# Weighted sums moved behind the bursts of scores in the attention part of a decoder layer

## The reference, cut to what matters

```python
x = layernorm(x + attn(x))        # 32 samples of 128 tokens, 1024 wide
x = layernorm(x + xattn(x, ctx))  # a 3-tap convolution gated by cosine similarities
x = layernorm(x + ffn(x))         # rank-16 experts mixed by a softmax router
# attn, 32 query heads over 8 key heads of 32 columns, for each sample:
q, k, v = x @ wq.T, x @ wk.T, x @ wv.T     # q and k are rotated by position
scores = q @ k.T / sqrt(32)                # causal mask
out = softmax(scores) @ v @ wo.T
```

## Time and profile before

| | us |
|---|---|
| median of three executions | 1433.07 |
| the profiled execution | 1434.46 |
| its span (first to last instruction) | 1432.60 |
| part 1, first loads and steps 0 to 2 (to 84.29) | 84.29 |
| part 1, steps 3 to 30, from a burst of scores at 84.29 to one at 714.38 | 630.09 |
| part 1, steps 31 to 33 (714.38 to 780.79) | 66.41 |
| part 2 (from 780.79 to the end) | 651.8 |

### The profile page before, as it was taken

One profiled execution on the slowest core, in us unless ns is written; L12 is line 12 of the kernel. 1 busy time (PEld: TensorE's weight loads), 2 busy tenths in 40 slices (PEclk: granted clock), 3 DMA queues, 4 the chain that ended last, 5 costly groups with the idle time before them and its releaser, 6 DMA issues. The chain is left out here.

```text
span 1432.6 us, 32298 instructions
## 1 busy us (share of the span) xinstructions
PE 1368.6 (96%) x8288; PEld 1060.1 (74%) x8288; DVE 1091.2 (76%) x3869; ACT 932.3 (65%) x3258; POOL 983.9 (69%) x936
## 2 busy tenths in 40 slices
PE   6999999999999999999985899999999999999995
PEld 4777777777777777777753688888888888888873
DVE  5677777777777777777775487788887788887774
ACT  5688878788787877878775354555554455554543
POOL 2777777777677776777764666777776777776763
PEclk9999999999999999999996999999999999999997
DMA  7345445454444544445466856655666766766651
GB/s 242 97 126 157 128 135 150 119 157 121 139 152 118 152 123 145 147 121 152 120 193 175 204 150 167 174 148 161 164 156 165 174 150 160 165 153 164 161 118 45
DMA packets 108861, 213.03 MB, mean 149 GB/s; under 512 B 26640, under 2 KB 32272, under 8 KB 108816
## 3 DMA queue, kind: packets, MB, share of 16 engines
q1 hardware_dynamic: 108624, 212.25, 53.9%
q10 hardware_dynamic: 192, 0.26, 0.1%
HBM read 131.83 MB, written 34.47 MB: 116 GB/s over the span
## 5 line engine op out<-in xcount | busy, mean ns | idle before, releaser
L435 PE MATMUL wo_ps<-weights,halves 128*128 128x512 f32 x2304 | 573.8, 400 | 11.8 <-DVE weights L614 11.7
L435 PEld LDWEIGHTS wo_ps<-weights,halves 128*128 128x128 f32 x2304 | 423.9, 190 | 128.6 <-issue 34.6
L697 ACT ACTIVATE pexp<-sm,smin 128x128 f32<-128x128 f32 x1024 | 398.8, 393 | 122.8 <-DVE smin L565 120.9
L1056 PE MATMUL wo_ps<-weights,halves 128*128 128x512 f32 x1488 | 400.9, 402 | 2.6 <-DVE yz L1159 2.6
L827 POOL TENSOR_TENSOR pn<-pexp,prec 128x512 f32<-128x512 f32 x256 | 268.6, 1049 | 146.9 <-DVE prec L572 146.9
L1409 POOL TENSOR_TENSOR prods<-prod,prods 128x512 fp32r<-128x512 f32 x192 | 259.3, 1358 | 134.5 <-ACT prods L1303 129.5
L1056 PEld LDWEIGHTS wo_ps<-weights,halves 128*128 128x128 f32 x1488 | 273.4, 190 | 61.6 <-issue 4.3
L565 DVE CUSTOM_DVE_ANT_0 sm<-s_ps,mask_t 128x128 f32<-128x128 f32 x1024 | 231.7, 281 | 78.7 <-PE s_ps L465 77.5
L1303 ACT CAST prods<-prod 128x512 fp32r<-128x512 f32 x192 | 118.8, 621 | 165.8 <-DVE prod L1193 129.2
L1193 DVE TENSOR_TENSOR prod<-att,x 128x512 f32<-128x512 f32 x192 | 187.0, 989 | 12.2 <-DMA att<-sim_scratch 9.7
L697 ACT ACTIVATION_READ_ACCUMULATOR pexp<-sm,smin 128x1 f32 x1024 | 194.8, 190 | 0.0
(11 more groups left out here) (99 smaller groups left out, 1661.2 us busy)
## 6 DMA issues: line engine op xcount, KB each, us to landing
att<-sim_scratch SPq DMA_DIRECT2D x192, 252.0 KB
pt<-blocks SPq DMA_DIRECT2D x636, 64.0 KB, 2.0
ctx_t<-in_ctx SPq DMA_DIRECT2D x32, 576.0 KB, 4.6
raw<-in_xT SPq DMA_DIRECT2D x32, 512.0 KB, 3.8
raw<-ot_scratch SPq DMA_DIRECT2D x32, 512.0 KB, 6.7
xn<-in_x SPq DMA_DIRECT2D x32, 512.0 KB, 7.4
out<-late SPq DMA_DIRECT2D x32, 512.0 KB, 6.2
ot_scratch<-ot SPq DMA_DIRECT2D x63, 256.0 KB, 2.1
```

Of the source, the lines that this page charges most:

```text
L435: mm = pe.matmul(qkv_ps[(par + g) % 2][:], xs[:, par, xl, k], w_sb[:, wl, g, k], start=(k == 0 and n == 0), stop=(k == KT - 1 and n == 2))
L697: ins = nc.scalar.activation(pexp[:, c % 2, i * P:(i + 1) * P], sm[:, c % 2, i * P:(i + 1) * P], ACT.Exp, bias=smin[:, c % 2, i:i + 1], sc ...
L1056: mm = pe.matmul(wo_ps[n][:], os_t[:, par, ol, k], wo_sb[:, wl, k, n * BANK:(n + 1) * BANK], start=(k == 0 and m == 0), stop=(k == KT - 1 ...
```

## The change

`weigh` moves. Half 0 of sample b goes from slot 9 to slot 13, directly behind the second burst of scores; half 1 goes from slot 17 to slot 1 of the next step, directly behind the first burst (there the sample is c = t-3). In steps 32 and 33 half 1 stays at slot 17, and half 0 is at slot 13 in them too.

ScalarE reads the sums one place later: at chunk 3 it reads half 1 of c (before: half 0 of b), at chunk 6 half 0 of b (before: half 1 of b). In steps 32 and 33 it reads half 1 at chunk 7.

SyncE's list follows: `move_v` of sample a goes from the end of step a to the next step, behind the loads of the next sample and its context; the store of half 0 goes to the end of the step and that of half 1 behind `move_p(b, 1)` of the next step; a wait for half 0 of the sums now stands ahead of the store of the context sums.

```diff
@@ move_p(a, u), on SyncE
-            wait(sp, pv_done, after(a - 1, NU, u + 1))
+            if u == 1:
+                wait(sp, pv_done, after(a - 1, NU, NU))
@@ step(t, par), on SyncE
+            a, b, c = t - 1, t - 2, t - 3
+            if at_step(t, 1):
+                move_v(0, 0)
...
+            if valid(a) and not at_step(t, 1):
+                move_v(a, 1 - par)
             if valid(b):
                 move_p(b, 1)
-                wait(sp, ot_read, after(b, NU, 1))
-                sp.dma_start(ot_dram[b, :, 0:BANK], ot[:, 0]).then_inc(ot_out[0], 16)
+            if valid(c) and not at_step(t, LAST):
+                store_later_half(c)
             if at_step(t, LAST):
                 store_own()
...
+            if valid(a):
+                wait(sp, pv_done, after(a - 1, NU, 1))
             if valid(t):
                 wait(sp, sq_done, after(t, 1, 1))
...
-                move_v(t, par)
...
-            if valid(b) and not at_step(b, B - 1):
-                wait(sp, ot_read, after(b, NU, 2))
-                sp.dma_start(ot_dram[b, :, BANK:D], ot[:, 1]).then_inc(ot_out[1], 16)
+            if valid(b):
+                wait(sp, ot_read, after(b, NU, 1))
+                sp.dma_start(ot_dram[b, :, 0:BANK], ot[:, 0]).then_inc(ot_out[0], 16)
+            if at_step(t, B):
+                store_later_half(b)
@@ step(t, par), on TensorE
-                if valid(b):
-                    if s == 9:
-                        weigh(b, par, 0)
-                    if s == 17:
-                        weigh(b, par, 1)
+                if s == 1 and valid(c) and not at_step(t, LAST):
+                    weigh(c, 1 - par, 1)
+                if s == 1 + NJ * PERIOD and valid(b):
+                    weigh(b, par, 0)
+                if s == 17 and (at_step(t, B) or at_step(t, LAST)):
+                    weigh(b, par, 1)
@@ step(t, par), on ScalarE
-                if p == 6 and at_step(t, LAST):
+                if p == 7 and at_step(t, LAST):
                     move_last_row()
...
-                if p == 3 and valid(b):
+                if p == 3 and valid(c) and not at_step(t, LAST):
+                    read_ot(c, 1)
+                if p == 6 and valid(b):
                     read_ot(b, 0)
-                if p == 6 and valid(b):
+                if p == 7 and (at_step(t, B) or at_step(t, LAST)):
                     read_ot(b, 1)
                 if p == 6 and valid(t):
                     copy_k(t, par)
```

More of the change, by code:

```diff
@@ L309, in move_p, with store_later_half @@
                                  ).then_inc(p_in[u], 16)
+        def store_later_half(b):
+            wait(sp, ot_read, after(b, NU, 2))
+            sp.dma_start(ot_dram[b, :, BANK:D], ot[:, 1]).then_inc(ot_out[1], 16)
         def load_later(n):
@@ L373, in step @@
         def step(t, par):
-            a, b = t - 1, t - 2
+            a, b, c = t - 1, t - 2, t - 3
+            if at_step(t, 1):
+                move_v(0, 0)
             if valid(t + 1):
```

## The result

The changed kernel took 1449.02 us (median of five, 1446.89 to 1450.13), the kernel before 1432.07 beside it: ratio 1.0123 (95% interval 1.0106 to 1.0140). It is slower, as forecast, but by 17.0 us and not by 9.6. A second set of five gave 1449.75 against 1432.48, ratio 1.0126 (1.0104 to 1.0147).

The account below looks back on a forecast made before the run. TensorE, never idle in steps 3 to 30, bounds the kernel. First steps -0.2, 28 steps +7.2, steps 31 to 33 +0.5, end of part 1 +2.05: +9.6 on 1433.07 gives 1442.7 us, range 1434 to 1449 (8 in 10).

Parts of the forecast that it names:

- TensorE's own list: TensorE's work in one step without waits: moving both halves of the sums changes it by 2x - 0.68, or -0.28 us.
- x: Distance from the last score matmul to the first of the moved sums: taken as 0.20 us, bounds 0.03 and 0.33.
- The stall at slot 22: Query transposes wait for ScalarE's key copy, which comes 1.00 later: TensorE idle 0.52 us a step, step 22.76.
- `copy_q`: ScalarE's query copy ahead of the first burst of scores: 0.70 us of cover left, costs nothing.
- the barrier: End of part 1: last sums' store now issued behind the similarities, its landing awaited before part 2: +2.05 us, once.
- `move_v` behind the context load: Values queue behind two large loads in each step; VectorE waits 0.5 to 1.0 us for them, hidden, price 0.
- a second wait at T1: Rival: values land later, chunk 3's mask delays the second burst of scores; 1451 us; dearer case, chance 0.14.
- First steps, -0.2: Start of part 1: sums leave a stretch where TensorE waited anyway, values leave the next load's way: -0.2 us at step 3.
- Steps 31 to 33, +0.5: End of part 1: SyncE issues the reload of `ot_scratch` 0.54 later, ScalarE waits for it: +0.5 us.

Follow-up runs that it names:

- the version without waits: Changed kernel with two v_new buffers, key copy at chunk 5, last store ahead of the similarities, next sample's rounding behind the query copy: 1421.27 us.
- the kernel with two buffers: Changed kernel with v_new in two buffers, so VectorE's copy need not wait for the last transfer out of it: 1440.78 us.

## Why the prediction was right in sign and too low

*TensorE's own list, 2x - 0.68 with x = 0.20.* Right. x is 0.20 (325.48 less the last score at 325.28) in all 56 bursts of steps 3 to 30, and the version without waits has 22.213 where 22.22 was forecast. The Trainium skill, "TensorEngine Tiling (Array Packing)", section Key Properties, says that a change of tiling mode drains the engine. The 0.20 us agree with it, against the 0.03 between two scores of one burst. (The argument that every change between full and partial array shows 0.17 more was too wide: behind transposes it is 0.17, behind 512-wide matmuls 0.10, as the prediction's own lines have it.)

*The stall at slot 22.* Right in place, cause and chain; 0.44 and not 0.52, because the transposes follow the key copy by 0.42, and not by the 0.51 read in step 31. The quiet step is 22.72 against 22.76. One piece of the chain did not have to be there: with the read of 0.47 us ahead of the key copy moved, the same late group 1 makes no stall.

*`copy_q` and the barrier.* Right: 1.24 ahead of T0, so it costs nothing (334.86 to 336.10); +2.08 against +2.05.

*`move_v` behind the context load: "Hidden, price 0".* This step failed. The mechanism was written down, its size was not. I took a landing at T1 + 20.1 or a little later and a wait of 0.5 to 1.0 us. The context load was taken to land 4.5 us behind its issue, as before; it lands 5.1 behind it now, and the values 0.56 behind that, as estimated. They are issued 4.1 behind T0 and land 5.1 later, at T1 + 11.7 + 4.1 + 5.1 = T1 + 20.9, and the wait is 1.3 on average. That mean is within the cover, which by the rival "a second wait at T1" ends at T1 + 21.4, or at a wait of 1.8, and by the traces at 1.6. But the waits reach 2.2, and what each has beyond the cover is paid in full: +0.09 a step. A mean was set against a cover where the spread decides.

*First steps, -0.2.* This failed by the same cause: +2.7 in the first profile and +1.7 in the second. I looked at who leaves the way of a load, and not at a step in which SyncE is late anyway: there the values are issued at 63.35, behind both loads, and VectorE would take them over at 66.14 (the time in the kernel with two buffers), 2.8 us later, which no landing of 5 us can meet. For what comes with it the prediction had no term: around the wait of 4.14 us the granted clock falls to 0.50, which costs another 2.5 us. With two buffers on both sides the first steps are level: 42.94 to 44.54 in three kernels with both halves moved, 43.88 and 45.21 in two without.

*Steps 31 to 33, +0.5.* It is +1.0 to the similarities (66.13 from T0 of step 31, 65.09 before): T1 of step 31 is 1.7 us later against T0, and half of that is made up behind it.

The sum over the profiles: first steps +2.7, steps +8.6 (28 x 0.22 for the stall less the shorter list, 28 x 0.09 for the values, where 28 x 0.26 was forecast), steps 31 to 33 +1.0, barrier +2.1, part 2 +0.1, that is +14.5. Ahead of T0 of step 1 the profile of before was 2.1 later (T0 of step 1 at 38.03; the thirteen others lie at 35.6 to 36.9), so that the spans differ by 12.4 only. The medians differ by 17. The remaining 2.5 us have no place in a trace: the profiled run of after was its fastest, and part 2 varies from 651 to 654 us between kernels that do the same there. The mean granted clock of each execution, which is on record, points at TensorE's clock: it was 0.979 to 0.982 in the five of the changed kernel and 0.981 to 0.986 in the 14 of the kernel before beside the first experiments, but 0.980 in the profiled one of before. In the second set of the changed kernel the shortest execution (1445.14 us) has 0.982 and the longest (1453.30) 0.978. The two go together; that the clock is the cause of these 2.5 us is not shown.

## What to carry to other kernels

Price a move on a saturated engine (one that is never idle) twice: once by the engine's own list, and once for every wait on its way, as release time less arrival time by the list. Moving work from between a release and its use shortens the list and the cover by the same amount, and an unrelated operation queued ahead of the releasing one (here a read of 0.47 us) can be the whole stall. Where a transfer's cover is thin, a mean landing time is no bound: put small transfers that are waited for ahead of large ones, or give the buffer a second copy, before judging the move itself.

## What the runs showed of the hardware

A 128 KB transfer queued behind 1.1 MB of loads on one queue lands 5.1 us behind its issue (4.1 to 6.1 in steps 3 to 30), ahead of them 2.1. From the last score matmul to the first of the sums, with the array going from 32 rows to 32 columns, it is 0.20 us, as before between transposes and sums. From the start of a 128x256 copy on ScalarE to the matmul that waits for it, it is 0.42 us, in single steps near either end of part 1 0.49 to 0.52; for a 128x512 copy 0.61 to 0.69. In both profiles of the changed kernel TensorE's granted clock went from 1.00 to 0.50 in or just behind its idle time of 4.1 to 4.2 us in step 2, for 6.8 us in one and 3.4 in the other, at 2.5 and 1.5 us of cost (14.35 and 13.36 us against 11.82).
